# Graph network of four layers on one core: sort without messages and histogram, first and third layer with x stationary

## The chip, the cores and the metric

The kernel runs on one core of one Trainium2 chip. The metric is the device time of one execution in microseconds. TensorE (PE; PEld is its weight load), VectorE (DVE), ScalarE (ACT), GpSimd (POOL) and the DMA queue of SyncE (SP) work side by side and meet at semaphores.

## The reference

Four message-passing layers over 6250 nodes of 128 features and 200,000 edges. Each layer's result is added to x and layer-normalised.

```python
# layer 0: relation embedding, mean over incoming edges
msg = (x[src] + rel_emb[type64]) @ W_msg.T + b_msg
agg = segment_sum(msg, dst) / maximum(segment_sum(1, dst), 1)
x = layernorm(x + x @ W_self.T + b_self + agg)
# layer 1: four-head attention, sums over edges with row = src, col = dst
val_exp = exp(val - mx[src]) * edge_weight
agg = segment_sum(val_exp * h_neigh[dst], src) / segment_sum(val_exp, src)
x = layernorm(x + (norm(h_self) + norm(agg)) / 2)
# layer 2: two edge types, each with its own weights
msg = where(type2 == 0, x[src] @ W_data.T + b_data, x[src] @ W_control.T + b_control)
x = layernorm(x + relu(segment_sum(msg, dst) + x @ W_self.T + b_self))
# layer 3: symmetric normalisation with self loops
x = layernorm(x + segment_sum(norm * (x @ W.T + b)[dst], src))
```

## The kernel before, in words

Nodes lie in 49 tiles (NT) of 128. A sort routes the edge records into chunks of 128, one for each pair (source tile, destination tile), 49 x 49, and one spare chunk for each source tile (NX = 50 columns in a row of `recs`). No layer gathers: from the 128 records of a chunk, DVE compares place numbers with an iota and gets one-hot matrices, PE multiplies two of them into a 128x128 count table of the pair, ACT copies the table out of PSUM, and PE multiplies table and node features into the sums. A layer has seven batches of seven tiles (G7, NB); after each batch its `node` steps (dense products, norms) are dealt out over the next batch's loop, the last batch's stand behind the loop.

- Sort (block ahead of `aggregate_shared`, L234 to L723): 226 units of up to 32 chunk columns, 49 of the first level and 177 behind. In a unit DVE makes one-hots `O` (L582), `M` (L688), `rank` (L592), values `VO` (L701) and the permutation `PM` (L87); PE counts (L463, L466) and routes (L482); ACT copies (`R` L367, `place` L376, `recs`). Beside it run: the out-degree histogram (`sources`, `sides`: ten columns in each of the first 157 units), and from unit 77 on `linear`, which turns x into messages x @ W_msg.T + b_msg, split into three bf16 parts in `X`.
- Relation, layer 0 (`aggregate_own`, k = 1): for each of 50 destination steps 8 loops over 6 or 7 source tiles; per chunk a table matmul (L1765), a 64-column relation matmul (L1862) and a 384-column matmul with the table stationary and X moving (L1865). The tables go to HBM over a ring of 4.
- Weighted, layer 1 (k = 2): 49 rows x 8 loops; per chunk three table matmuls (L1761) and a float32 sum of 132 columns in two passes (L1867). The spare chunk has a table of its own: 50 tables in a row.
- Typed, layer 2 (k = 3): tables of all edges come back from HBM, ACT turns them into fp32r (L1711); per chunk one new table (L1765), one 258-column and one 256-column fp32r matmul, both with the table stationary (L1867, L1882). The last batch's steps, the splits of the new x into `Xr`, and `split_last_states` stand behind the loop.
- Plain, layer 3 (`aggregate_plain_turned`): here x is stationary and seven tables of one source tile stream, 448 columns at a time (L2123).

Of the kernel before, what the change touches and what calls it, by code (L numbers as in the profile page):

```python
# [22 lines left out]

# [13 lines left out]
def gnn_four_layers_kernel(nc, t, out):  # L37
# [13 lines left out]

# [10 lines left out]
    QUARTERS = RING = 4  # L62
    LONGEST = max(NT * (r + 1) // QUARTERS - NT * r // QUARTERS for r in range(QUARTERS))
    tab_d = nc.dram_tensor("tables", (NX * QUARTERS, P, LONGEST * P), BF16, kind="Internal").ap()

    with ExitStack() as ctx:
# [47 lines left out]
        relx = sb("relx", [P, 3, P], BF16)  # L114
        relw = sb("relw", [REL, P + 1], F32)
# [3 lines left out]
        ROW = 2 * P + 2  # L119
# [7 lines left out]
        spare = early[:, 2 * RC:]  # L127
# [7 lines left out]
        with ExitStack() as c1:  # L135
            raw = recs[:, :, :].bitcast(I32).rearrange("p c w -> p (c w)")
            psrc, pdst, esrc, edst = [raw[:, j * COLS:(j + 1) * COLS] for j in range(4)]
            turn_at = recs[:, :, :].rearrange("p c w -> p (c w)")[:, RC * 4 - COLS:RC * 4]
            ts_p = recs_h.rearrange("p c h -> p (c h)")[:, RC * 8 - 4 * COLS:RC * 8 - 2 * COLS].rearrange("p (c b) -> p c b", b=2)
# [21 lines left out]
            side = sb("side", [P, 2, 16, P + 2], BF16, c1)  # L161
            ts_hot = sb("ts_hot", [P, 2, 16, NTE], BF16, c1)
            dego = sb("dego", [NT, P], F32, c1)
            degx = sb("degx", [NT, P + 1], F32, c1)
            degs = sb("degs", [P, NT], F32, c1)
            valid = sb("valid", [P, 2], F32, c1)
            total_of = sb("total_of", [P, 1], F32, c1)
            junk = side[:, :, :, :].rearrange("p h n w -> p (h n w)")
            WT = sb("WT0", [P, 2, P], F32, c1)
            wnat = sb("wnat0", [P, 3, P], F32, c1)  # L170
            relT = sb("relT0", [P, REL], F32, c1)
            bias = sb("bias0", [P, 2, P], F32, c1)
            rel_r = sb("rel_r0", [REL, P], F32, c1)
            xT = sb("xT0", [P, P], F32, c1)
            msg = sb("msg0", [P, P], F32, c1)
# [3 lines left out]
            pL = ps("pL", [P, 3, P], c1)  # L179
# [4 lines left out]
                     "s_outhot", "s_side", "s_dego", "s_outadd", "s_deg", "s_tp0", "s_xt0", "s_y0", "s_lin0", "s_link0", "s_wt0", "s_valid", "s_total", "s_kind")  # L184
            (loads, pads, consts, tri_made, prep, fields, blanks, weighed, s_pad, s_load, s_xin, s_stored, turned, wt_made,
             s_dup, s_hot, s_cnt, s_look, s_mul, s_rank, s_more, s_pair, s_val, s_perm, s_out, s_ev,
             s_outhot, s_side, s_dego, s_outadd, s_deg, s_tp, s_xt, s_y, s_lin, s_link, s_wt, s_valid, s_total, s_kind) = [sem(n, c1) for n in names]
# [25 lines left out]
            SIDES = 10  # L213
            COUNTED = -(-COLS // SIDES)
            pieces_of = {n: (n * SIDES, min(SIDES, COLS - n * SIDES)) for n in range(COUNTED)}
            done_with = {u.d: n + 1 for n, u in enumerate(units) if u.level == 3}
            assert COUNTED < done_with[7] and 8 * TOP * NX * 8 <= RC * 8 - 4 * COLS
            LIN, LIN_AT = 7, A_N + 28
            assert LIN_AT + 3 * NT + 1 <= UN
            PREP, FIELDS, WEIGHED = 15, 9, 4  # L220
            PADDED = 96

            def slot_of(n):
# [1957 lines left out]
```

## Time and profile before

| | us |
|---|---|
| median of 3 runs | 4517.38 (4517.27 to 4522.35) |
| the profiled execution | 4517.95 |
| its span | 4516.2 |
| PE / PEld busy | 3879.5 (86%) / 3400.8 (75%) |
| DVE busy | 3899.9 (86%) |
| ACT busy | 2636.9 (58%) |
| POOL busy | 234.8 (5%) |

Busy time of an engine is the union of its instructions; neighbours on DVE and ACT overlap by about 0.08 us in the records, and matmuls overlap much more, since their ends are modelled. So PE is read by the distance from start to start. Shares over the whole span mix five stages with different limits; the rows below give them stage by stage.

### The profile page before, as it was taken

What the parts mean: (1) busy time and instruction counts of PE and PEld (TensorE: products, weight loads), DVE (VectorE), ACT (ScalarE), POOL (GpSimd) and SP (SyncE); (2) the same over time, 40 slices, a digit from 0 to 9 for tenths busy, and PEclk for the clock granted to TensorE, in tenths of its full rate; (3) what the DMA queues carried; (4) which work ended last, traced back from release to release, by engine and by line L of the source; (5) the groups of instructions that cost most, each with busy time, mean ns of one, the idle gap of its engine ahead of it and who ended that gap; (6) DMA issues with size and microseconds to landing.
All of it is one profiled execution on the core that took longest, in us unless ns stands there. A gap on an engine that the chain in (4) does not pass through costs nothing. (4 is left out here: it accounts for less than half of the span.)

```text
span 4516.2 us, 106596 instructions
## 1 busy us (share of the span) xinstructions
PE 3879.5 (86%) x43111; PEld 3400.8 (75%) x43112; DVE 3899.9 (86%) x6758; ACT 2636.9 (58%) x5471; POOL 234.8 (5%) x165
## 2 busy tenths in 40 slices
PE   3667777766679999995999999997999999969998
PEld 3556666555557666665999999997999999957776
DVE  8999999999988889986999999997666666669888
ACT  6878777843335555542333333333888888856776
POOL 1000001010100000000101011111000000000000
PEclk9989889989789999997999999998999999979999
DMA  3000000000013222220000000001333333300000
GB/s 106 1 1 2 1 2 2 2 2 1 2 51 122 112 109 114 108 108 2 2 2 2 2 2 2 2 2 34 106 98 97 98 97 97 97 5 5 10 9 9
DMA packets 92948, 183.53 MB, mean 41 GB/s; under 512 B 10329, under 2 KB 63781, under 8 KB 92322
## 3 DMA queue, kind: packets, MB, share of 16 engines
q1 hardware_dynamic: 91970, 174.17, 12.0%
q8 instruction: 351, 5.75, 0.5%
q10 hardware_dynamic: 480, 2.40, 0.2%
q14 instruction: 147, 1.20, 0.1%
HBM read 88.63 MB, written 87.90 MB: 39 GB/s over the span
## 5 line engine op out<-in xcount | busy, mean ns | idle before, releaser
L1720 ACT ACTIVATE gC<-qC 128x768 fp32r<-128x768 f32 (+3 forms) x792 | 653.4, 825 | 659.0 <-PE qC L1761 640.4
L87 DVE TENSOR_TENSOR g<-iota_own,recs 128x768 bf16<-128x768 bf16 (+1 forms) x1200 | 636.5, 560 | 177.2 <-PE qC L1765 171.1
L482 PE MATMUL pV<-VO,PM 128*128 128x98 bf16 (+4 forms) x6524 | 386.0, 225 | 326.8 <-issue 322.1
L1867 PE MATMUL qO<-A,gC 128*128 128x132 f32 x4900 | 637.0, 280 | 0.0
L482 PEld LDWEIGHTS pV<-VO,PM 128*128 128x128 bf16 x6524 | 356.4, 108 | 349.9 <-issue 348.9
L1867 PEld LDWEIGHTS qO<-A,gC 128*128 128x128 f32 x4900 | 581.3, 190 | 0.0
L1865 PE MATMUL qO<-terms,ring 128*128 128x384 bf16 x2450 | 523.7, 327 | 0.0
L1718 ACT ACTIVATE ring<-qC 128x768 bf16<-128x768 f32 (+1 forms) x400 | 328.8, 822 | 286.7 <-PE qC L1765 286.6
L87 DVE TENSOR_TENSOR PM<-iota_b,place 128x3584 bf16<-128x3584 bf16 (+1 forms) x226 | 469.8, 2079 | 14.7 <-ACT place L376 14.5
L414 ACT ACTIVATE side<-iota_b,recs 128x129 bf16<-128x129 bf16 x1568 | 475.6, 397 | 0.7 <-PE pD L492 0.7
L1862 PE MATMUL qO<-terms 128*128 128x64 bf16 x2450 | 470.2, 193 | 0.0
L87 DVE TENSOR_TENSOR places_hot<-iota_own,recs 128x896 bf16<-128x896 bf16 x700 | 403.1, 620 | 54.4 <-PE tC L2111 21.7
L2093 ACT ACTIVATE tables_r<-tC 128x896 fp32r<-128x896 f32 x350 | 320.7, 918 | 146.3 <-PE tC L2111 145.6
L1882 PE MATMUL qA<-Xr,kept_r 128*128 128x256 f32 x2450 | 386.8, 294 | 2.9 <-ACT kept_r L1711 2.9
L1711 ACT ACTIVATE kept_r<-sl_f 128x768 fp32r<-128x768 bf16 (+1 forms) x400 | 343.3, 858 | 77.2 <-PE qO L1867 63.2
L2123 PE MATMUL tO<-tables_r,Xr 128*128 128x448 f32 x1400 | 372.6, 388 | 9.0 <-ACT tables_r L2093 4.7
L1248 DVE TENSOR_TENSOR g<-sl_f 128x2304 bf16<-128x2304 bf16 (+1 forms) x262 | 369.9, 1412 | 0.2 <-PE qC L1761 0.2
L701 DVE TENSOR_TENSOR VO<-O,V 128x2744 bf16<-128x2744 bf16 (+3 forms) x226 | 362.5, 1604 | 3.6
L1867 PE MATMUL qO<-Xr,gC 128*128 128x258 f32 x2450 | 364.3, 285 | 1.1 <-ACT gC L1720 1.1
L1761 PE MATMUL qC<-g,sl_f 128*128 128x128 bf16 x4914 | 319.4, 220 | 47.9 <-DVE g L1248 46.9
L1865 PEld LDWEIGHTS qO<-terms,ring 128*128 128x128 bf16 x2450 | 239.2, 98 | 134.8 <-issue 0.7
L1761 PEld LDWEIGHTS qC<-g,sl_f 128*128 128x128 bf16 x4914 | 294.3, 98 | 59.4 <-DVE g L1248 54.6
(268 smaller groups left out, 6740.5 us busy)
## 6 DMA issues: line engine op xcount, KB each, us to landing
sl_f<-tables SPq DMA_DIRECT2D x350, 192.0 KB, 2.3
tables<-ring SPq DMA_DIRECT2D x150, 384.0 KB, 2.3
tables<-ring SPq DMA_DIRECT2D x50, 416.0 KB, 2.4
sl_f<-tables SPq DMA_DIRECT2D x50, 224.0 KB, 2.5
edges<-terms SPq DMA_DIRECT2D x1, 4312.0 KB, 13.5
B<-in_x SPq DMA_DIRECT2D x1, 2744.0 KB
out<-B SPq DMA_DIRECT2D x7, 392.0 KB
terms<-in_edge_type ACTq DMA_DIRECT2D x2, 686.0 KB
```

Source lines behind the costliest of these rows:

```text
L87: return v.tensor_tensor(o.rearrange("p n (a b) -> p n a b", b=2), (iota_own if own else iota_b)[:, at:at + w].rearrange("p (a b) -> p a b ...
L414: ins = act.activation(side[:, n % 2, j, 0:P + 1], iota_b[:, 0:P + 1], ACT.Sign, bias=turn_at[:, at + j:at + j + 1])
L482: mm = pe.matmul(pV[n % 2][:, g * row:(g + 1) * row].rearrange("p (f b) -> p f b", f=u.nf), PM[:, n % 2, col, :], values[:, :, col, :], st ...
L701: v.tensor_tensor(VO[:, n % 2, 0:cols * u.nf * u.w].rearrange("p (f n a b) -> p f n a b", b=2, a=u.w // 2, f=u.nf), where.unsqueeze(1).bro ...
L1248: ins = v.tensor_tensor(h1[:, par, 0:n, :, :].rearrange("p n s (a b) -> p n s a b", b=2), bare[Q % 3][:, 0:n, 1, :].rearrange("p n (a b) - ...
L1720: act.activation(Cs[:, u % 2, 0:n, :], pC[u % 2][:, 0:n, :], ACT.Copy).then_inc(s_cs, 1)
L1761: mm = pe.matmul(pC[u % 2][:, j, :], bare[G % 3][:, j, 0, :], h1[:, q % NHB, j, s, :], start=s == 0, stop=s == 2)
L1862: pe.matmul(pO[i % SUMS][:, parts * P:parts * P + P // 2], h2[:, q % NHB, j, :], h3[:, q % NHB, j, :], start=first, stop=last, skip_group_ ...
L1865: mm = pe.matmul(pO[i % SUMS][:, 0:width], table_j, x, start=False, stop=last, skip_group_check=True)
L1867: mm = pe.matmul(pO[i % SUMS][:, 0:width], table_j, x, start=first, stop=last)
L1882: mm = pe.matmul(pA[:, :], kept_r[:, q % 2, a - cut[q], :], Xr[:, a, 0:2 * P], start=a == 0, stop=a == NT - 1)
L2123: mm = pe.matmul(pO[:, h, 0:HW], Xr[:, b % NT, s * P:(s + 1) * P], table_h[:, h, :], start=b == 0 and s == 0, stop=b == NX - 1 and s == 1, ...
```

## The change

- Sort: `linear`, `relations`, `sources`, `sides` and `degrees` go. `X` holds x itself in three bf16 parts, made seven tiles at a time by ACT (`high_part`, `mid_part`) and POOL (`low_parts`). x @ W_self.T + b_self + x comes wholly from PE, and ACT copies it to `B`. The spare chunk of a row moves to its first column.
- Relation: new function with 343 units (7 batches x 49 source tiles). In a unit PE makes the tables of 7 destination tiles, the spare chunk adding into the first one's, streams them past `X` (three parts, stationary), and counts relations and types with 65-column matmuls. W_msg is applied to the sums in `node`, the relation counts times `relw` too. The out-degrees are summed by the ACTIVATE that copies the tables (`accum_out`).
- Weighted: 7 loops of 7 tiles in a row in place of 8; the spare chunk shares a table, so there are 49 sums in place of 50.
- Typed: like plain, with x (two fp32r parts) stationary; tables of all edges and of type 1 stream, 512 and 384 columns. The copies to fp32r are shared by DVE and ACT. The sums are already turned and go into the dense products as they are. The splits of batches 0 to 5 move into the loop of the last batch.
- Plain keeps its loop but for the column order. The table ring is 5 pieces of 224 KB. The SBUF reserve for dynamic DMA is 2048 bytes.

```diff
-                    def linear(n, step):
...
-                            v.tensor_tensor(msg[:, :], pL[:, 1, :], bias[:, 0, :], ALU.add).then_inc(s_lin, 1)
-                            v.tensor_tensor(own_x, own_x, pL[:, 2, :], ALU.add).then_inc(s_lin, 1)
...
-                        equal(v, ts_hot[:, n % 2, 0:cols, :], ts_p[:, at:at + cols, :], cols, NTE).then_inc(s_outhot, 1)
+                        gp.tensor_tensor(xrest[:, :, :], B[:, T, :], X[:, T, 0, :], ALU.subtract).then_inc(s_rest, 1)
+                        gp.wait_ge(s_mid, m + 1)
+                        gp.tensor_tensor(X[:, T, 2, :], xrest[:, :, :], X[:, T, 1, :], ALU.subtract).then_inc(s_low, 1)
...
+        def aggregate_relation_turned():
...
+                            equal_both_own(v, both_hot[:, U % 3, 0:n, :, :], places_of(chunk, n), n, P).then_inc(s_hot, 1)
...
+                            equal(v, rel_hot[:, K % 2, 0:n, 0:REL], rel_p[:, rel_at(m, a):rel_at(m, a) + n, :], n, REL, own=True).then_inc(s_rel, 1)
...
+                            act.activation(kept[U % RING].rearrange("p (n d) -> p n d", d=P), pC[U % 2][:, 0:G7, :], ACT.Copy, accum_out=sent[:, m, a:a + 1]).then_inc(s_cs, 1)
...
+                                for s in range(3):
+                                    mm = pe.matmul(pO[:, h, 0:(hi - lo) * P], X[:, a, s, :], of_half(kept[U % RING], h),
+                                                   start=a == 0 and s == 0, stop=a == NT - 1 and s == 2, skip_group_check=True)
...
+                                mm = pe.matmul(pR[:, to:to + DW], both_hot[:, U % 3, j, 0, :], rel_hot[:, K % 2, a % FOUR * n + j, 0:DW],
...
+                                        pe.matmul(pN[:, j - lo, :], A[:, m * G7 + j, 0:P], WTm[:, :], start=True, stop=False, skip_group_check=True)
+                                        mm = pe.matmul(pN[:, j - lo, :], RT[0:REL, j - lo, :], relw[:, :], start=False, stop=True, skip_group_check=True)
...
+        def aggregate_typed_turned():
...
+                            pe.wait_ge(s_kept[U % 2], U // 2 + 1) if whole else pe.wait_ge(s_cs, 2 * U + 2)
...
+                                for s in range(2):
+                                    mm = pe.matmul((pA if whole else pK)[:, h, 0:(hi - lo) * P], Xr[:, a, s * P:(s + 1) * P], of_half((all_r if whole else some_r)[:, U % 2, :], h),
...
+                        convert(0)
+                        for U in range(AHEAD):
+                            make(U)
...
+    nc = _bacc.Bacc("TRN2", target_bir_lowering=False, num_devices=1, dynamic_dma_scratch_size=2048)
```

DVE in the first level of the sort, one unit and the start of the next, before and then of the change:

```order
L701 TENSOR_TENSOR VO<-O,V 128x3584
L87 TENSOR_TENSOR PM<-iota_b,place 128x4096
L87 TENSOR_TENSOR ts_hot<-iota_b,recs 128x500
L688 TENSOR_TENSOR M<-O,R 128x448
L582 TENSOR_TENSOR O<-iota,V 128x448
L592 TENSOR_REDUCE rank<-M 128x32
```

```order
L656 TENSOR_TENSOR VO<-O,V 128x3584
L88 TENSOR_TENSOR PM<-iota_b,place 128x4096
L646 TENSOR_TENSOR M<-O,R 128x448
L606 TENSOR_TENSOR O<-iota,V 128x448
L616 TENSOR_REDUCE rank<-M 128x32
```

One row of six is gone. PE in the relation loop, before (the pair L1862 and L1865 stands once for each of 6 or 7 chunks) and then of the change, a whole unit and the start of a `node` step (rC and rO are the tables' and the sums' PSUM, rR the counts', sl_f the ring of tables, terms holds X):

```order
L1765 MATMUL qC<-terms,g 128x128 x6
L1862 MATMUL qO<-terms 128x64
L1865 MATMUL qO<-terms,ring 128x384
L1862 MATMUL qO<-terms 128x64
L1865 MATMUL qO<-terms,ring 128x384
```

```order
L1316 MATMUL rC<-both_hot 128x128 x7
L1328 MATMUL rO<-sl_f,terms 128x512 x3
L1328 MATMUL rO<-sl_f,terms 128x384 x3
L1343 MATMUL rR<-rel_hot,both_hot 128x65 x7
L1372 MATMUL rN<-ident_f,terms 64x128 x3
```

The narrow matmuls, which stood between wide ones, now stand seven in a row behind six wide ones.

## Rows read from the trace of the kernel before

**Rows 1.** Windows by stage: length, busy time and instructions of each engine, PE clock, DMA.
```profile
44.00:1301.00 1257.00, 873.00 (x11217) 734.06 (x11217) 1197.87 (x1797) 828.28 (x3020) 87.90 (x39) 0.89 0.03 8
...
1309.00:2026.00 717.00, 691.12 (x7733) 499.17 (x7733) 645.87 (x1655) 374.89 (x546) 0.00 (x0) 1.00 0.29 114
2026.00:2090.00 64.00, 12.44 (x45) 8.33 (x43) 30.94 (x48) 9.75 (x20) 9.32 (x6) 0.53 0.02 5
2090.00:3106.00 1016.00, 995.95 (x12250) 979.13 (x12250) 978.28 (x1014) 363.85 (x465) 106.01 (x96) 1.00 0.01 2
...
3134.00:3963.00 829.00, 823.11 (x7882) 797.20 (x7882) 533.15 (x1279) 673.73 (x951) 0.00 (x0) 1.00 0.36 99
3963.00:4017.00 54.00, 20.16 (x88) 14.29 (x88) 25.91 (x56) 16.66 (x32) 0.00 (x0) 0.61 0.00 1
```
**Rows 2.** Groups of DVE by line in 44 to 1301: busy, mean ns, idle before.
```profile
L688 DVE TENSOR_TENSOR M<-O,R 128x448 bf16<-128x448 bf16 (+2 forms) x226 | 83.9, 371 | 23.9 <-ACT R L367 23.7
...
L87 DVE TENSOR_TENSOR ts_hot<-iota_b,recs 128x500 bf16<-128x500 bf16 (+1 forms) x157 | 65.7, 419 | 0.0
L624 DVE TENSOR_TENSOR msg<-pL,bias 128x128 f32<-128x128 f32 x49 | 13.8, 283 | 3.7 <-PE pL L520 3.6
```
**Rows 3.** Timeline of DVE, a unit of the sort: start, length, instruction.
```profile
253.07 0.41 DVE L87 TENSOR_TENSOR ts_hot<-iota_b,recs 128x500 bf16<-128x500 bf16 x1
253.40 0.38 DVE L688 TENSOR_TENSOR M<-O,R 128x448 bf16<-128x448 bf16 x1
```
**Rows 4.** Timeline of PE in the sort, at full and at half clock.
```profile
1102.56 1.43 PE L482 MATMUL pV<-VO,PM 128*128 128x98 bf16 x28 [2.81 <-issue]
...
1285.28 2.12 PE L482 MATMUL pV<-VO,PM 128*128 128x84 bf16 x28 [2.56 <-issue]
...
1287.52 1.82 PE L466 MATMUL pR<-O,ones_b 128*128 128x364 bf16 x13
```
**Rows 5.** Timeline of GpSimd and VectorE where both work in the sort.
```profile
844.27 4.37 POOL L308 TENSOR_SCALAR beyond<-recs 128x200 bf16<-128x200 bf16 x1 [73.84 <-ACT recs L405]
...
1290.94 1.07 DVE L688 TENSOR_TENSOR M<-O,R 128x392 bf16<-128x392 bf16 x1
```
**Rows 6.** Timeline of PE in the relation loop, of PEld in the sort.
```profile
1708.27 0.19 PE L1862 MATMUL qO<-terms 128*128 128x64 bf16 x1
...
1708.46 0.52 PE L1765 MATMUL qC<-terms,g 128*128 128x128 bf16 x6
1708.81 0.19 PE L1862 MATMUL qO<-terms 128*128 128x64 bf16 x1
...
605.09 1.15 PEld L482 LDWEIGHTS pV<-VO,PM 128*128 128x128 bf16 x28 [0.91 <-issue]
```
**Rows 7.** Groups of DVE in the weighted stage, both one-hots of 6 and 7 chunks.
```profile
L93 DVE TENSOR_TENSOR sl_f<-iota_own,recs 128x1536 bf16<-128x1536 bf16 x194 | 185.9, 958 | 16.7 <-PE qC L1761 15.2
...
L93 DVE TENSOR_TENSOR sl_f<-iota_own,recs 128x1792 bf16<-128x1792 bf16 x66 | 71.7, 1087 | 7.3 <-PE qC L1761 6.5
```
**Rows 8.** Timeline of PE: dense product; typed loop, table to table; plain loop.
```profile
3972.00 1.16 PE L1792 MATMUL qN<-nWT,nxT 128*128 128x128 f32 x8
...
3403.44 0.50 PE L1765 MATMUL qC<-g 128*128 128x128 bf16 x6
...
3405.26 0.51 PE L1765 MATMUL qC<-g 128*128 128x128 bf16 x6
...
4290.13 0.56 PE L2111 MATMUL tC<-places_hot 128*128 128x128 bf16 x7
4290.51 1.06 PE L2123 MATMUL tO<-tables_r,Xr 128*128 128x448 f32 x4
4291.41 0.56 PE L2111 MATMUL tC<-places_hot 128*128 128x128 bf16 x7
```
**Rows 9.** Timeline behind the typed loop: VectorE adds the last dense product.
```profile
3985.11 0.54 DVE L1524 TENSOR_TENSOR A<-A,qN 128x384 f32<-128x384 f32 x1
```
**Rows 10.** DMA issues of the page: KB each, us from issue to landing.
```profile
sl_f<-tables SPq DMA_DIRECT2D x350, 192.0 KB, 2.3
```

More of the change, by code:

```diff
@@ L315, in _ @@
+                    gp.wait_ge(s_kind, n_kind)
                 @block.scalar
@@ L1045, in aggregate_own @@
-                if mode == "typed":
-                    kept = [sl_f[:, b * most * P // 2:(b + 1) * most * P // 2].bitcast(BF16).rearrange("p (n d) -> p n d", d=P) for b in range(RING)]
-                    kept_r = sb("kept_r", [P, 2, most, P], F32R, c)
-                if mode != "relation":
-                    Cs = sb(f"gC{name}", [P, 2, most, P], F32R if mode in ("plain", "typed") else cdt, c)
-                total = sb(f"total{name}", [P, 1, P], F32, c) if mode in ("relation", "plain") else None
@@ new lines, in node @@
+                            if slot == 43:
+                                after()
+                                step(v.tensor_tensor(Bt, Hn[:, :, :], W1[:, :, :], ALU.add))
+                        make_relations(0)
+                        for U in range(AHEAD):
+                            make(U)
+                        for U in range(UNITS):
+                            m, a = unit(U)
+                            if a == 0 and m > 0:
+                                close(m - 1)
+                            if U + AHEAD < UNITS:
+                                make(U + AHEAD)
+                                m2, a2 = unit(U + AHEAD)
+                                if a2 % FOUR == 0:
+                                    make_relations(pack_of(m2, a2))
+                            if m > 0:
+                                node(m - 1, a)
+                            elif a == 6:
+                                rows()
@@ L1891, in relations @@
-                        def relations(i):
-                            pe.wait_ge(s_reln, i + 1)
-                            if i >= 1:
-                                pe.wait_ge(s_total, 2 * i)
-                            pe.matmul(pE[:, 0:P + 1], rel_n[:, :], relw[:, :], start=True, stop=True).then_inc(s_relm, 1)
-                        table(0, 0)
-                        batch(0, None)
-                        for o in range(1, NB):
-                            batch(o, o - 1)
-                        if mode == "relation":
-                            turn_relations(TN - 1)
-                            relations(TN - 1)
@@ new lines, in node @@
+                                if slot == when + 4:
+                                    project(use + 2, hf, 1)
+                        table(0)
+                        for U in range(UNITS):
+                            m, a = unit(U)
+                            if U + 1 < UNITS:
+                                table(U + 1)
+                            sums(U)
+                            relations(U)
+                            if m > 0:
+                                node(m - 1, a)
+                            elif a == 7:
+                                weights()
@@ L1909, in softmax_weights @@
+                        for slot in range(44):
+                            node(NB - 1, slot)
         def softmax_weights():
@@ new lines, in _ @@
+                        for U in range(2):
+                            make(U)
+                        for U in range(UN):
+                            i, q = unit(U)
+                            m, slot = i // G7, U % (G7 * NQ)
+                            if U + 2 < UN:
+                                make(U + 2)
+                            if U + 2 == UN:
+                                recode()
+                            if q == 0 and i > 0:
+                                take(i - 1)
+                            if m > 0:
+                                node(m - 1, slot)
+                            else:
+                                degrees(slot)
```

1861 lines of the change are left out of this document (962 added, 899 removed).

## The prediction

> **What bounds the kernel now.** I read the windows by stage first, since the five stages have different limits, then the groups and waits of the sort, then PE's timeline in each loop. The windows [rows 1] say: in the sort (44 to 1301 us) DVE is busy 1198 of 1257 us, PE 873, ACT 828: DVE sets the pace, and 59 us of it is waiting, the largest part for `R` from ACT, 24 us [rows 2], that is for the chain PE route, PE count, ACT copy. In the relation loop (717 us) PE shows 691 us and DVE 646; in the weighted loop (1016 us) PE 996 and DVE 978; in the typed loop (829 us) PE 823 and DVE only 533. Behind the relation and the typed loop stand 64 and 54 us in which no engine is half busy: the last batch's steps, one after the other. The reader is to see that every stage has one engine to save on: DVE in the sort, PE in the typed loop, both at once in the other two.
>
> **The sort.** The histogram's one-hot is made in 157 units at 419 ns [rows 2]; neighbours overlap, and from its start to the next instruction's it is 0.33 us [rows 3], so 157 x 0.33 = 52 us. `linear` takes seven instructions of DVE for each of 49 tiles; the first is 283 ns [rows 2], with an overlap of 0.08 (0.41 - 0.33, [rows 3]) 0.20 net, and the short ones among them less, so 343 x 0.19 = 65 us. The few steps on relations and degrees give 3 us. Together 120 us of the engine that bounds. PE loses 1568 small matmuls and ACT as many `side` copies, neither of which is the bound, so that is worth nothing by itself. What is late next is the chain through PE. At full clock it routes 28 columns in 1.43 us, at half clock in 2.12, and counts in 1.82 there [rows 4]. At half clock 2.12 + 1.82 + the first count 0.5 + ACT's copy 0.5 + some 0.1 us for each of four hand-overs makes 5.3; a DVE unit of the later levels shrinks to about 4.5. So each unit at half clock now costs up to 0.8 us of new waiting. PE's clock is 0.89 in this window [rows 1], which is the half level 22% of the time: 226 x 0.22 x 0.8 = 40 us at most beside what is waited already, 0 at least; I take 15, since the units with waiting today already hold part of it. The seven 896-element copies twice on ACT (0.9 us each) stand in its slack, and PE's one matmul more per tile too. Sort: -120 + 15 = -105.
>
> GpSimd gets 14 subtractions of 896 floats beside DVE. Where both worked, one `M` took 1.07 us in place of 0.38 [rows 5, 3], while GpSimd's own instruction stretched to 4.37 us: it is mostly GpSimd that gives way. 14 x 0.7 = 10 us at most; I take 2, in the 15 above. The Trainium skill (SBUF — State Buffer, Who interferes with whom) states that a VectorE instruction with two inputs in SBUF and a GpSimd instruction that reads SBUF exclude each other for a whole instruction. If GpSimd always came first that would be a rival, below.
>
> **The relation loop.** Now 343 units of 7 tiles. Tables: six take from 1708.46 to 1708.81 [rows 6], 0.058 each, so 0.41 us. X stationary: 3 x (512 + 384) = 2688 columns; today 448 columns with two weight loads take 0.19 us (1708.27 to 1708.46), 0.424 ns a column, so 1.14 us. Seven 65-column matmuls: no trace of such a row of them. Bounds are the column rate, 0.027 each, and the table's 0.058; the nearest is the sort's weight loads, 28 in 1.15 us [rows 6], (1.15 - 0.10) / 27 = 0.039, which I take: 0.27 us. Unit 1.82 us (1.74 to 1.96), x 343 = 624 us, and 5 for the spare columns. `node` on PE: a dense product of float32 is (1.16 - 0.28) / 7 = 0.126 per pass, two passes [rows 8], 0.25 us; a batch has 14 of them today, and 14 more with `WTm` and `relw`, 7 transposes more, bias rows: 9.5 us, x 6 = 57. Sum 686 us. Today the same count gives 400 x 1.52 + 31 + 18 for the 50 relation products = 657, against 717 measured: 60 us lost to DVE's bursts. DVE drops: per unit one one-hot of 1792 (1.087 us [rows 7], net 1.0) and a quarter of another, 1.25 us, with node some 550 us of 700; but its node slots of 2.3 us against PE's 1.82 still come four at a time. I take 25 us lost (5 to 60). ACT's copy of 0.92 us and reading the accumulator, which no row shows, have 0.9 us of slack. Loop 686 + 25 = 711: -6 (-50 to +40).
>
> Behind the loop stand `keep`, the added transposes and products before the first norm: about 13 us in place of 7, and GpSimd clears one more array before: +7.
>
> **The weighted loop.** 343 pairs of DVE instructions replace 392. By rows [rows 7] 256 elements more cost 0.129 us, so what an instruction costs beside its elements is net 1.087 - 1792 x 0.000504 - 0.08, about 0.10 us; 98 fewer are 10 us, and PE's 49 sums fewer 49 x 0.23 = 11 us. Both engines that bound shrink by the same: -10 (-15 to -2).
>
> **The typed loop.** Today six tables and twelve sums of 256 to 258 columns go from 3403.44 to 3405.26 [rows 8]: 1.82 us. After: four sums of 512 and four of 384 for seven tiles. In the plain loop four sums of 448 take 0.90 us (4290.51 to 4291.41), 0.226 each with the change from bf16 to fp32r in it. Both rows fit a cost of 0.055 for that change, once for a unit, and 0.211 for 448 columns, 0.12 for 257: 0.48 ns a column, so 0.242 and 0.180. Four pairs 1.69, the change 0.055, seven tables 0.39: 2.10 us after rounding down, since the trace of the plain loop has single steps of 0.205. Bounds: the bf16 rate 0.424 gives 1.91, 0.226/448 gives 2.20. x 343 = 720, spare columns 3, `node` on PE 9 us a batch, 54, waits of the short buffers 8: 785. So -44 (-105 to +5). DVE has 1.0 for one-hots, half a convert and node, about 1.7 us of 2.1; ACT two halves and half a convert, 1.5: both hidden.
>
> Behind it: today the chains of turn and product last until 3985.11 [rows 9], 22 us, with six splits queued into the 10 us behind. After, two chains of transpose and three products, about 10 us, and no splits but one: 54 - 19 = 35 us, -19 (-10 to -26). Its start waits for the first table, since `convert(0)` stands ahead of `make`: the DMA's 2.3 us [rows 10] and the copy, +3.
>
> **Sum.** -105 - 6 + 7 - 10 - 44 - 19 + 3 = -174. The plain stage and the softmax between are not changed. The profiled execution took 4517.95, 0.6 above the median of the runs, which is nothing here; 4518 - 174 = 4344. I say 4342.
>
> **Rivals.**
> - The TensorE clock stays low in the sort. With less work PE idles more, and at half clock the chain of 5.3 us becomes the unit in most units: 226 x about 0.5 more = 110 us, and the sort gains about 10. 4440. For it: the clock already falls with some 30% idle. Against: at half clock PE is busy nearly throughout, and the half level lasts 3 or 4 us at a time today, in which DVE keeps on. 6%.
> - The relation loop gets worse: narrow matmuls at 0.058, DVE's bursts at today's 60 us: 343 x 0.13 + 35 = +80. 4422. For: seven narrow ones in a row have never been seen here. 8%.
> - GpSimd first: all 14 subtractions hold DVE for their length. By DVE's kind of float32 work on 896 elements at 1.1 us and GpSimd two to four times slower, 14 x 3 = 42 us more: 4384. This is what the page's rule on the shared port would do at its worst. 5%.
> - Slower than before: the tables' DMAs go one by one. Both turned loops need one piece of 224 KB for each unit, in 1.82 and 2.10 us, while landing takes 2.3 us for 192 KB [rows 10]. If the smaller reserve let only one be in flight, with issue 0.3 and landing 2.4 a unit would take 2.7 us and more; it decides from 1.82 on, costs 2 x 343 x 0.75 = 510 us, less the slack, and gives 4850. For it: the diff lowers that reserve. Against: the queue is of the hardware kind and was at 114 GB/s with 0.29 of the engines [rows 1]; the new rate is 120. 3%.
> - It doesn't do what it says: the typed loop stays bound by something else at 829. 4386. 4%, as DVE and ACT would both have to be 20% above my count.
>
> **Chances.** Forecast 4342, 74%; the rivals 6, 8, 5, 3 and 4%. Adding the parts' better and worse ends independently gives about -55 and +60 around the forecast; the worse cases of the rivals reach to 4440. Range 4285 to 4405, which leaves out about 2 in 10. A difference under 0.2% (9 us) is no change that the runs can tell. Faster by more: 95%; within it: 1%; slower: 4%, the DMA case and what I haven't thought of.
>
> **What would show it.** In the profile after: the sort ends near 1195 us; a DVE unit of its first level takes 5.27 us in place of 5.60 (start of `M` to start of `M`); the relation loop's unit is near 1.85 us between `node` steps and its 65-column matmuls start 0.04 us apart; the typed unit is 2.1 us, its 512-column sums start 0.24 apart; typed to plain 35 us; the weighted loop about 1006. I am wrong if DVE's wait for `R` grows past 60 us, if ACT in the relation loop waits for `tables`, or if the one-hots come late to the tables.

## The result and the profile after

The changed kernel takes 4362.97 us in the median of four runs (4352.71 to 4366.67), the kernel before 4517.59. The ratio on record is 0.9652, 95% interval 0.9634 to 0.967; the two medians divided give 0.9658. The forecast was 4342 with a range of 4285 to 4405. The profiled execution is the shortest of the four, 4352.71 with a span of 4351.0, so what it lost against before in span is 165.2 us, ten more than the medians say.

First the windows by stage of the changed kernel, with the columns of [rows 1] (start and end, length, busy time and instructions of PE, PEld, DVE, ACT, POOL, clock, DMA share, GB/s):

```profile
44.00:1185.70 1141.70, 757.41 (x9742) 640.47 (x9742) 1099.54 (x1280) 418.87 (x1510) 144.03 (x98) 0.90 0.03 8
...
1200.30:1930.90 730.60, 697.91 (x7404) 479.95 (x7404) 557.57 (x678) 395.07 (x802) 105.93 (x89) 1.00 0.29 110
...
2002.70:3003.00 1000.30, 980.38 (x12152) 966.94 (x12152) 969.88 (x917) 350.60 (x417) 81.39 (x96) 1.00 0.01 2
...
3035.20:3820.40 785.20, 783.19 (x5643) 652.97 (x5644) 543.95 (x765) 524.11 (x978) 0.00 (x0) 1.00 0.34 101
```

For before I cut the sort at the start of its last routing matmul and the loops at their first and last matmul in the same way:

```profile
44.00:1297.80 1253.80, 871.74 (x11213) 733.08 (x11213) 1196.63 (x1791) 827.78 (x3016) 86.20 (x36) 0.89 0.03 8
1309.10:2026.10 717.00, 691.22 (x7733) 499.19 (x7733) 645.84 (x1655) 374.89 (x546) 0.00 (x0) 1.00 0.29 114
...
3134.10:3962.60 828.50, 823.03 (x7882) 797.20 (x7882) 532.77 (x1276) 673.73 (x951) 0.00 (x0) 1.00 0.36 99
```

Stage by stage, in us of the two profiled executions, beside what was forecast:

| from ... to | before | after | difference | forecast |
|---|---|---|---|---|
| start to the first table of the relation loop | 1309.1 | 1200.3 | -108.8 | -105 |
| relation loop | 717.0 | 730.6 | +13.6 | -6 |
| behind it | 64.0 | 71.8 | +7.8 | +7 |
| weighted loop | 1015.9 | 1000.3 | -15.6 | -10 |
| weighted to typed | 28.1 | 32.2 | +4.1 | +3 |
| typed loop | 828.5 | 785.2 | -43.3 | -44 |
| behind it | 54.7 | 32.8 | -21.9 | -19 |
| plain stage | 498.9 | 497.8 | -1.1 | 0 |
| sum | | | -165.2 | -174 |

Seven of the eight rows are within 6 us, and the typed loop is right to one. The relation loop alone is on the wrong side, by 20 us: it got longer. And the first row is right as a sum and wrong inside, as the experiments below show.

Now the groups of DVE in the sort of the changed kernel (busy, mean ns, idle before and its releaser), the answer to [rows 2]:

```profile
L88 DVE TENSOR_TENSOR PM<-iota_b,place 128x3584 bf16<-128x3584 bf16 (+1 forms) x226 | 472.0, 2088 | 0.0
L656 DVE TENSOR_TENSOR VO<-O,V 128x2744 bf16<-128x2744 bf16 (+3 forms) x226 | 371.9, 1645 | 5.1
...
L646 DVE TENSOR_TENSOR M<-O,R 128x448 bf16<-128x448 bf16 (+2 forms) x226 | 90.4, 400 | 21.9 <-ACT R L396 21.7
```

And the same engine before, two groups that [rows 2] does not hold:

```profile
L87 DVE TENSOR_TENSOR PM<-iota_b,place 128x3584 bf16<-128x3584 bf16 (+1 forms) x226 | 469.8, 2079 | 14.7 <-ACT place L376 14.5
L701 DVE TENSOR_TENSOR VO<-O,V 128x2744 bf16<-128x2744 bf16 (+3 forms) x226 | 362.5, 1604 | 3.6
```

Two things are to be seen. The same instructions have become longer: M 90.4 us in place of 83.9, VO 371.9 in place of 362.5. And a wait is gone: PM waited 14.5 us for ACT's `place`, now nothing. The wait of M for `R`, on which I had put the loss, is 21.7 us in place of 23.7.

PE in the relation loop, timeline (start, length, instruction), a unit and one `node` step:

```profile
1317.04 1.30 PE L1328 MATMUL rO<-sl_f,terms 128*128 128x512 bf16 x6
1318.17 0.39 PE L1343 MATMUL rR<-rel_hot,both_hot 128*128 128x65 bf16 x7
1318.40 0.46 PE L1378 MATMUL rN<-WTm,A 128*128 128x128 f32 x2
1318.79 0.48 PE L1379 MATMUL rN<-relw,terms 64*128 64x128 f32 x2
1319.21 0.49 PE L1378 MATMUL rN<-WTm,A 128*128 128x128 f32 x2
...
1320.88 0.56 PE L1316 MATMUL rC<-both_hot 128*128 128x128 bf16 x7
1321.28 1.30 PE L1328 MATMUL rO<-sl_f,terms 128*128 128x512 bf16 x6
1322.41 0.38 PE L1343 MATMUL rR<-rel_hot,both_hot 128*128 128x65 bf16 x7
1322.63 0.55 PE L1316 MATMUL rC<-both_hot 128*128 128x128 bf16 x7
```

A unit without `node` takes 1.75 us (1320.88 to 1322.63): 0.40 for tables, 1.13 for the six wide sums, 0.22 for the seven narrow ones, all inside the bounds of the forecast. Between `node` products it is different: each group of two passes starts 0.41 to 0.42 us behind the one before, so one pass costs 0.207 us on average, where the forecast had 0.126. PE in the typed loop, timeline:

```profile
3301.24 0.56 PE L2064 MATMUL rC<-both_hot 128*128 128x128 bf16 x7
3301.62 1.06 PE L2076 MATMUL rK<-some_r,Xr 128*128 128x512 f32 x4
3302.51 0.98 PE L2076 MATMUL rA<-all_r,Xr 128*128 128x512 f32 x4
3303.34 0.56 PE L2064 MATMUL rC<-both_hot 128*128 128x128 bf16 x7
```

A unit is 2.10 us, as forecast. Last, GpSimd and VectorE where one of GpSimd's new subtractions runs, timeline of the changed kernel:

```profile
365.96 1.95 POOL L314 TENSOR_TENSOR xrest<-B,terms 128x896 f32<-128x896 f32 x1 [327.54 <-ACT terms L450]
366.09 0.55 DVE L616 TENSOR_REDUCE rank<-M 128x28 f32<-128x392 bf16 x1
366.56 2.80 DVE L656 TENSOR_TENSOR VO<-O,V 128x2744 bf16<-128x2744 bf16 x1
```

VO takes 1.57 us where GpSimd is still. It began at 366.56, GpSimd's instruction ended at 367.91, and 2.80 is longer by 1.23: VectorE stood until about then. The reduction before it, which reads one tensor, kept its 0.55. Over the 14 subtractions the instruction with two inputs beside each is 1.04 to 1.69 us longer, 18.9 us in all.

### The profile page after: what moved, and what is told of

Same layout as the page of the kernel before. It is cut to its first block and busy times, and to the rows that moved or that the text cites. A ratio compares the mean times of both kernels' runs of the same rounds, so it can differ in the third digit from the quotient of the medians.

```text
span 4351.0 us, 94545 instructions
## 1 busy us (share of the span) xinstructions
PE 3717.3 (85%) x38991; PEld 3134.1 (72%) x38992; DVE 3708.3 (85%) x4644; ACT 2074.6 (48%) x4187; POOL 381.5 (9%) x320
## 5 line engine op out<-in xcount | busy, mean ns | idle before, releaser
L94 DVE TENSOR_TENSOR both_hot<-iota_own,recs 128x1792 bf16<-128x1792 bf16 (+1 forms) x686 | 756.8, 1106 | 252.2 <-PE rR L1343 142.5
L1690 ACT ACTIVATE gC<-qC 128x896 f32<-128x896 f32 x343 | 314.8, 918 | 647.9 <-PE qC L1710 647.9
L2034 ACT ACTIVATE some_r<-rC 128x512 fp32r<-128x512 f32 (+1 forms) x686 | 336.4, 543 | 253.1 <-PE rC L2064 252.6
L1328 PE MATMUL rO<-sl_f,terms 128*128 128x512 bf16 (+1 forms) x2058 | 446.6, 353 | 4.0 <-ACT sl_f L1294 2.4
L1294 ACT ACTIVATE sl_f<-rC 128x896 bf16<-128x896 f32 x343 | 314.1, 916 | 279.6 <-PE rC L1316 279.4
L656 DVE TENSOR_TENSOR VO<-O,V 128x2744 bf16<-128x2744 bf16 (+3 forms) x226 | 371.9, 1645 | 5.1
L1528 DVE TENSOR_TENSOR g<-sl_f 128x2688 bf16<-128x2688 bf16 (+1 forms) x229 | 363.6, 1588 | 0.2 <-PE qC L1710 0.2
L2076 PE MATMUL rK<-some_r,Xr 128*128 128x512 f32 (+1 forms) x1372 | 363.2, 386 | 0.0
L2076 PE MATMUL rA<-all_r,Xr 128*128 128x512 f32 (+1 forms) x1372 | 342.0, 371 | 1.9 <-DVE all_r L1835 1.9
L507 PE MATMUL pR<-O,ones_b 128*128 128x392 bf16 (+16 forms) x2644 | 301.3, 267 | 0.0
L507 PEld LDWEIGHTS pR<-O,ones_b 128*128 128x128 bf16 x2644 | 242.7, 105 | 79.8 <-issue 20.1
```

The lines of the kernel that those rows point to most:

```text
L94: return v.tensor_tensor(o.rearrange("p n k (a b) -> p (n k) a b", b=2), iota_own[:, 0:w].rearrange("p (a b) -> p a b", b=2).unsqueeze(1). ...
L507: mm = pe.matmul(pR[n % 2][:, (j + 1) * row:k].rearrange("p (m r) -> p m r", r=row), ones_b[:, :], O[:, n % 2, j * row:(j + 1) * row].unsq ...
L656: v.tensor_tensor(VO[:, n % 2, 0:cols * u.nf * u.w].rearrange("p (f n a b) -> p f n a b", b=2, a=u.w // 2, f=u.nf), where.unsqueeze(1).bro ...
L1328: mm = pe.matmul(pO[:, h, 0:(hi - lo) * P], X[:, a, s, :], of_half(kept[U % RING], h), start=a == 0 and s == 0, stop=a == NT - 1 and s == ...
L1528: v.tensor_tensor(h1[:, U % 2, 0:n, :, :].rearrange("p n s (a b) -> p n s a b", b=2), bare[U % 3][:, 0:n, 1, :].rearrange("p n (a b) -> p ...
L2034: act.activation(of_half(some_r[:, U % 2, :], h).rearrange("p (n d) -> p n d", d=P), pC[Q % 3][:, 0:hi - lo, :], ACT.Copy).then_inc(s_cs, 1)
```

## Experiments

Differences are of medians. Runs of the changed kernel are read against its own repeat, runs of the kernel before against the kernel before beside them. The runs stood on three chips, and the kernel before took 4517.67 us beside after_again and the three n_ runs, 4518.34 beside s_low, s_kind, b_noside and b_nohot, and 4519.54 beside the rest. So a difference to the repeat on another chip holds to some 2 us at best.

**after_again: the changed kernel once more.**

> The changed kernel once more, so that the three next to it are read against it on the same chip: 4353 to 4367 us as in its first four runs. Relation loop 730 us, from the first table's matmul to the last narrow one.

Measured 4362.63 us (4359.66 to 4366.91); ratio 0.9659 (0.9646 to 0.9672). The relation loop took 730.5 us, all later stages agree to 1 us but for the step from typed to plain (34.6 in place of 32.8), and the sort was 6.2 us longer than in the first profile. So of the 7 us between these two profiles 6 are variation in the sort.

**n_padded and n_grouped: why a `node` product costs 0.41 us.** The first lets the products with relw run over 128 rows, in the old order (the add that fills relw keeps to its first 64 rows, which isn't shown):

```diff
-        relw = sb("relw", [REL, P], F32)
+        relw = sb("relw", [P, P], F32)
...
+                        v.memset(relw[REL:P, :], 0.0)
+                        v.memset(RT[REL:P, :, :], 0.0)
...
-mm = pe.matmul(pN[:, j - lo, :], RT[0:REL, j - lo, :], relw[:, :], start=False, stop=True, ...)
+mm = pe.matmul(pN[:, j - lo, :], RT[:, j - lo, :], relw[:, :], start=False, stop=True, ...)
```

> The products with relw run over all 128 rows (64 of them zero on both sides), in the old order, alternating with WTm. Theory S (rows change): passes fall from 0.207 to 0.126 us, 28 products by 0.16 us by 7 batches = -31 us at most where PE is what bounds, -20 to -30. Theory A (accumulation into the same region) and theory P (fixed price): 0.

The second changes only the order, in each half of a batch. It changes the sums that are formed in that bank too; only its time is used.

```diff
                                     for j in range(lo, hi):
                                         pe.matmul(pN[:, j - lo, :], A[:, m * G7 + j, 0:P], WTm[:, :], start=True, stop=False, ...)
+                                    for j in range(lo, hi):
                                         mm = pe.matmul(pN[:, j - lo, :], RT[0:REL, j - lo, :], relw[:, :], start=False, stop=True, ...)
```

> The 14 pairs of products of node in the relation loop (A by WTm with 128 rows, RT by relw with 64 rows) stand in pairs and take 0.413 us each in the trace, 0.207 for each of the two passes, while the dense products that follow each other take 0.126 for a pass. Here all products with WTm of a half come first, then all with relw. Theory S (the change between 128 and 64 rows costs, since the next weights can't load beside the running product): a batch has 28 products of which 24 no longer follow a change, each 0.16 us cheaper, 3.9 less four starts left, about -2 to -2.5 us a batch, -13 to -17 us in all. Theory A (accumulating behind a write to the same PSUM region costs): the same here. Theory P (such a product simply costs 0.41, whatever stands before it): 0.

n_padded: 4344.77 us (4340.72 to 4348.98), -17.9; n_grouped: 4347.45 (4342.77 to 4349.19), -15.2; both 0.9621 (0.9608 to 0.9634). Theory S had said -20 to -30 for the first, which it misses, and -13 to -17 for the second. PE in n_padded, timeline:

```profile
1314.60 0.46 PE L1380 MATMUL rN<-WTm,A 128*128 128x128 f32 x2
1314.90 0.39 PE L1381 MATMUL rN<-relw,terms 128*128 128x128 f32 x2
1315.13 0.39 PE L1380 MATMUL rN<-WTm,A 128*128 128x128 f32 x2
1315.35 0.39 PE L1381 MATMUL rN<-relw,terms 128*128 128x128 f32 x2
```

Each group of two passes starts 0.22 to 0.23 us behind the one before, 0.112 for a pass, in the same order and with twice the rows. That puts theory A (a price of adding to the same region) out, and also a fixed price for a product that adds. It leaves a rival: a pass over 64 rows might be dear in itself, and n_padded has none. PE in n_grouped settles that, timeline:

```profile
1325.31 0.91 PE L1378 MATMUL rN<-WTm,A 128*128 128x128 f32 x6
1326.15 0.93 PE L1380 MATMUL rN<-relw,terms 64*128 64x128 f32 x6
1327.01 0.56 PE L1316 MATMUL rC<-both_hot 128*128 128x128 bf16 x7
```

Six passes over 64 rows in a row take 0.86 us, hardly more than six over 128 (0.84): within the row they too start 0.112 us apart. So it is the change that costs, and once for each change: two passes behind a change take 0.41 us in place of 0.22, which is 0.19 us, or 0.09 on average for a pass. The weight loads show where it goes, PEld in the changed kernel and then in n_padded:

```profile
1318.79 0.29 PEld L1379 LDWEIGHTS rN<-relw,terms 64*128 64x128 f32 x2
```

```profile
1314.79 0.30 PEld L1381 LDWEIGHTS rN<-relw,terms 128*128 128x128 f32 x2
```

Behind a change of rows the load starts together with its matmul (1318.79, as in the rows above); without one it starts 0.11 us ahead of it (1314.79 against 1314.90), beside the matmul that still runs.

Counted so, a batch has 14 changes, none in n_padded and 4 in n_grouped: 98 by 0.19 are 18.6 us and 70 by 0.19 are 13.3. From the first table of the relation loop to the start of the weighted loop n_padded is 16.3 us shorter than the repeat and n_grouped 13.4. Both expectations had counted a batch's 28 passes as 28 products, so that n_grouped came out within its range by luck. The loop itself shrank from 730.5 to 716.6 us in n_padded, and what stands behind it from 72.1 to 69.6. In n_grouped a pass costs 0.14 on average.

**n_deep: the idle time of PE in the relation loop.**

```diff
-                both_hot = sb("both_hot0", [P, 3, G7 + 1, 2, P], BF16, c)
+                both_hot = sb("both_hot0", [P, 4, G7 + 1, 2, P], BF16, c)
...
-            AHEAD, FOUR = 2, 4
+            AHEAD, FOUR = 3, 4
```

(and the buffer's index modulo 4, the wait for its release one unit later)

> Four buffers of both_hot in place of three in the relation loop, and VectorE one unit further ahead. PE idles 33 us in this loop, in a batch 0.7 us in slot 12, 1.3 in slot 36 and 1.1 in slot 44, where VectorE's steps of node are in a row. Theory B (bursts longer than the lead): the lead grows by a unit of 1.74 us, the three gaps close nearly, -6 x 2.8 = -17 us (-10 to -20). Rival (VectorE is late for lack of throughput over the stretch, or held by its own wait for PE's products): at most -4 us.

4338.47 us (4327.84 to 4341.41), -24.2; 0.9598 (0.9585 to 0.9611). What PE waited for in the relation loop, of the changed kernel and of n_deep (us, times, longest):

```profile
PE rC L1316 <- DVE both_hot L94: 38.7, 32, 12.1
PE rO L1328 <- ACT sl_f L1294: 2.4, 6, 0.4
```

```profile
PE rC L1316 <- DVE both_hot L94: 16.7, 13, 11.9
PE rO L1328 <- ACT sl_f L1294: 8.6, 12, 1.2
```

The first 12 us of each are the way into the loop. Without them the idle time falls from 29 to 13 us. The whole gain is past the -10 to -20 of theory B, which went by the idle time that the profile shows. The loop is 24.1 us shorter, more than the idle time that went: the rest stands in the row of narrow matmuls, which from start to next start take 92.3 us in the changed kernel and 84.6 here. A wait shorter than the modelled length of the last matmul (0.19 us) is not told as idle. The lead was too short for VectorE's steps of `node`; its throughput was not the limit (557 of 730 us busy).

**s_low, s_kind: which of GpSimd's new work holds VectorE.**

```diff
-                        gp.tensor_tensor(xrest[:, :, :], B[:, T, :], X[:, T, 0, :], ALU.subtract).then_inc(s_rest, 1)
+                        gp.memset(xrest[:, :, :], 0.0).then_inc(s_rest, 1)
...
-                        gp.tensor_tensor(X[:, T, 2, :], xrest[:, :, :], X[:, T, 1, :], ALU.subtract).then_inc(s_low, 1)
+                        gp.memset(X[:, T, 2, :], 0.0).then_inc(s_low, 1)
```

> The changed kernel, in which GpSimd's 14 subtractions of 896 floats (the middle and low parts of X) are writes of zeros, so the middle and low parts are left out. VectorE's five instructions of a sort unit are 22 us longer in sum after the change than before (M 90.4 against 83.9 us, VO 371.9 against 362.5, PM 2.2, the first step on over-full groups 3.3). Theory L (it is the subtractions that hold VectorE): the sum falls back by 15 to 20 us. Theory K (it is GpSimd's 48 small additions to the relation numbers): by at most 5 us. Total -15 or -5 us against 4363.

```diff
-                        for a in range(n):
-                            gp.tensor_tensor(later[:, :, lo + a, :, :], ... , ALU.add).then_inc(s_kind, 1)
+                        gp.memset(later[:, :, lo:hi, :, :].rearrange("p m a c b -> p m (a c b)"), 0.0).then_inc(s_kind, 1)
```

> The changed kernel, in which GpSimd's 49 small additions that lay out the relation numbers of batches 1 to 6 are seven writes of zeros, so these relation numbers are left out. Theory K: VectorE's sum in the sort falls by 10 to 20 us. Theory L: by at most 5.

s_low: 4343.50 us (4341.11 to 4345.68), -19.1; 0.9613 (0.9597 to 0.9629). s_kind: 4368.41 (4365.48 to 4372.42), +5.8; 0.9668 (0.9652 to 0.9684). VectorE in the sort of s_low:

```profile
L656 DVE TENSOR_TENSOR VO<-O,V 128x2744 bf16<-128x2744 bf16 (+3 forms) x226 | 362.8, 1605 | 5.1
...
L646 DVE TENSOR_TENSOR M<-O,R 128x448 bf16<-128x448 bf16 (+2 forms) x226 | 85.5, 378 | 27.1 <-ACT R L396 27.0
```

With GpSimd's subtractions gone, VO is back at its time of before. It is the 14 wide subtractions and not the 49 small additions. Theory L stands: beside GpSimd's writes of zeros no VectorE instruction of s_low is longer than elsewhere. That s_kind came out 6 us slower was expected by neither theory. The intervals of its ratio and of the repeat's overlap, so this may be noise; in its profile VectorE waits 35 us for `R` in place of 24, and PE is at half clock for 290 us of the sort in place of 253. Why that should be so stays open.

**s_dve, s_pieces: the same subtractions elsewhere.** s_dve gives the two lines, unchanged but for the engine, to VectorE behind `PM`, at units 2 and 7 of each eight.

```diff
+                            m, when = divmod(n - SPLIT_AT, 8)
+                            if 0 <= m < NB and when == 2:
...
+                                v.tensor_tensor(xrest[:, :, :], B[:, T, :], X[:, T, 0, :], ALU.subtract).then_inc(s_rest, 1)
```

> The changed kernel with the 14 subtractions of X's parts on VectorE (after PM of units 2 and 7 of each eight) in place of GpSimd. In the profile each of GpSimd's takes 1.9 us and the VectorE instruction beside it is 1.1 to 1.7 us longer, 19 us in sum. Theory L (GpSimd's instruction holds VectorE's two-input instruction nearly for its whole length): on VectorE itself they cost 14 x 1.0 = 14 us, so 5 us less than now in the sort, 4350 to 4362. If GpSimd's had cost nothing, as my prediction had it: 14 us more, 4377.

s_pieces leaves them with GpSimd in seven pieces each:

```diff
+                        for i in range(G7):
+                            ins = gp.tensor_tensor(xrest[:, i:i + 1, :], B[:, m * G7 + i:m * G7 + i + 1, :], X[:, m * G7 + i:m * G7 + i + 1, 0, :], ALU.subtract)
+                        ins.then_inc(s_rest, 1)
```

> The changed kernel with each of GpSimd's 14 subtractions in seven of 128 floats. Theory L1 (the port passes at the end of each instruction of either engine, so a short one holds VectorE shortly, and VectorE's next goes on): VectorE's longest delay falls from 1.7 to about 0.3 us, but up to seven of them follow each other, sum 7 to 19 us in place of 19, total -5 (-12 to 0). Theory L2 (the two simply share reads by halves): no change in VectorE's sum.

s_dve: 4356.60 us (4351.97 to 4357.93), -6.0; 0.964 (0.9627 to 0.9653). s_pieces: 4352.09 (4349.96 to 4353.93), -10.5; 0.963 (0.9617 to 0.9643). On VectorE, the busiest engine of the stage, the subtractions seem to cost less than on the idle GpSimd: a subtraction takes 1.08 us there, and VectorE is busy for 1096 us of the sort in place of 1102 in the repeat. But the intervals of s_dve and the repeat overlap, and so do those of s_dve and s_pieces. s_pieces alone is clear of the repeat. The timeline of s_pieces has two kinds of stretch, first this one:

```profile
365.80 15.11 POOL L315 TENSOR_TENSOR xrest<-B,terms 128x128 f32<-128x128 f32 x7 [327.02 <-ACT terms L454]
366.40 1.56 DVE L660 TENSOR_TENSOR VO<-O,V 128x2744 bf16<-128x2744 bf16 x1
...
367.89 2.01 DVE L88 TENSOR_TENSOR PM<-iota_b,place 128x3584 bf16<-128x3584 bf16 x1
```

Here it is GpSimd that waits: seven pieces take 15.11 us, and VO and PM keep their 1.56 and 2.01. It is the only group of seven like this. The other 13 take 6.0 to 9.2 us, and VectorE is held in each:

```profile
388.85 6.63 POOL L319 TENSOR_TENSOR terms<-xrest,terms 128x128 bf16<-128x128 f32 x7 [7.94 <-ACT terms L460]
389.47 0.58 DVE L650 TENSOR_TENSOR M<-O,R 128x392 bf16<-128x392 bf16 x1
...
392.42 2.24 DVE L88 TENSOR_TENSOR PM<-iota_b,place 128x3584 bf16<-128x3584 bf16 x1
```

M takes 0.34 elsewhere and PM 2.01, so each is 0.23 or 0.24 longer. Over all 14 groups up to six instructions in a group are longer, none by more than 0.24 us, and the sum is 13.1 us in place of 18.9. That is theory L1 with its numbers (up to seven short delays of some 0.3, 7 to 19 us in sum); L2 (no change in VectorE's sum) is out. The 5.8 us saved on VectorE are about half of the 10.5 in the median; for the rest no run shows a cause. Nor does one show why the first group left VectorE alone.

**b_noside, b_nohot, b_both: the two halves of the histogram, in the kernel before.**

```diff
-                        for j in range(cols):
+                        for j in range(cols if n < 2 else 1):
                             ins = act.activation(side[:, n % 2, j, 0:P + 1], iota_b[:, 0:P + 1], ACT.Sign, bias=turn_at[:, at + j:at + j + 1])
```

> The kernel before, with one of ten side copies of ACT in each histogram unit after the second (about 1400 of 1568 left out, so the histogram is wrong), all VectorE and PE instructions as they are. My prediction counted ACT's part of the histogram at nothing: 4517. Rival theory: ACT's queue makes VectorE wait for place, 14.5 us before, which is gone after the change; then VectorE's wait before PM falls from 14.7 to under 3 us and the time to about 4505.

```diff
-                        equal(v, ts_hot[:, n % 2, 0:cols, :], ts_p[:, at:at + cols, :], cols, NTE).then_inc(s_outhot, 1)
+                        equal(v, ts_hot[:, n % 2, 0:(cols if n < 2 else 1), :], ts_p[:, at:at + (cols if n < 2 else 1), :], cols if n < 2 else 1, NTE).then_inc(s_outhot, 1)
```

> The kernel before, with VectorE's one-hot of the histogram cut to one column in each unit after the second (so the histogram is wrong). VectorE bounds the sort: 155 x (0.33 - about 0.10) = 36 us less, 4481. If the chain PE to ACT bounded instead: about 4510.

> The kernel before, with both cuts to the histogram: ACT's side copies (alone -18 us) and VectorE's one-hot (alone -13 us where VectorE had 30 us less to do), so the histogram is wrong. Theory C (the two engines are links of one cycle, VectorE's saving was eaten by waiting for ACT's place and R): together more than the sum, -40 to -50. Theory H (half clock: VectorE's saving is eaten by PE's chain at 1.2 GHz): the sum or less, -25 to -31.

The first expectation is met (4505 of the rival theory, not 4517). The second is not: 4481 was expected, and its other case, the chain PE to ACT with 4510, came nearer. b_noside: 4500.63 us (4495.45 to 4502.92), -17.7; 0.9958 (0.9941 to 0.9975). b_nohot: 4505.48 (4504.36 to 4507.9), -12.9; 0.997 (0.9958 to 0.9981). b_both: 4478.77 (4477.1 to 4483.82), -40.8; 0.991 (0.9897 to 0.9924). VectorE's `PM` in b_noside, the window of b_both's sort, and VectorE's waits in the sort of b_nohot and then of b_both (us, times, longest):

```profile
L87 DVE TENSOR_TENSOR PM<-iota_b,place 128x3584 bf16<-128x3584 bf16 (+1 forms) x226 | 470.3, 2081 | 0.2 <-ACT place L376 0.2
```

```profile
44.00:1257.70 1213.70, 859.50 (x11212) 721.67 (x11213) 1163.50 (x1788) 444.81 (x1623) 70.81 (x36) 0.90 0.03 8
```

```profile
DVE M L688 <- ACT R L367: 32.9, 44, 2.6
DVE PM L87 <- ACT place L376: 17.6, 38, 0.9
```

```profile
DVE M L688 <- ACT R L367: 26.9, 34, 2.6
DVE msg L624 <- PE pL L520: 6.0, 13, 1.2
```

Taking ACT's copies away gave 17.7 us, though ACT had been busy for only 828 of 1254: VectorE's wait for `place` is gone, and its idle time (length minus busy, sort) fell from 57 to 38 us. Taking 30 us of work from VectorE gave 12.9, since its idle time rose to 72 us. Both together gave 40.8, more than the 30.6 of the two apart, with the idle time at 50. The total is at the low edge of theory C and 10 us beyond theory H, but by the intervals of the three ratios the difference between 40.8 and 30.6 is itself uncertain by some 11 us; the sorts of the profiles, 40.1 us shorter against 19.7 and 14.6, put it at 6. And the larger part of what came back does not hang on ACT's copies: without them, from b_noside to b_both, VectorE lost 33 us of work and the sort only 20, with M's wait for `R` growing from 19 to 27 us. So the two halves of the histogram do act on each other, by a few us, and the largest part of the waiting that ate VectorE's saving is for `R`. What makes `R` late (PE's clock, PE's work or ACT's order) these runs don't separate.

**best: three edits at once.** relw and RT over 128 rows, four buffers, the subtractions on VectorE, each as above.

> Three edits to the changed kernel at once: relw and RT padded to 128 rows, four buffers of both_hot, the 14 subtractions on VectorE. The first two gave -18 and -24 us against 4362.6; they are in one loop, but one saves PE's work and the other PE's waiting, so they add: 4320; with the third 4315 (4305 to 4325). If VectorE becomes the bound of that loop once PE is faster, only -30: 4332.

4313.64 us (4309.33 to 4317.01); 0.9543 (0.953 to 0.9556), against 0.9659 (0.9646 to 0.9672) of the changed kernel beside the same kernel before. Its relation loop takes 690.8 us (1202.1 to 1892.9). The gains add, as 4315 had it, and this is the fastest of all kernels here. s_pieces in place of s_dve wasn't tried in this combination.

## Why the prediction was right, point by point

- **Typed loop, -44:** -43.3. The terms hold one by one. From start to next start the 2744 wide sums on record cost 0.218 us on average, eight of them 1.74 (forecast 1.69 and 0.055 for the change of type), seven tables 0.39 (0.39). PE is busy 783 of 785 us, ACT and DVE are both hidden with 524 and 544.
- **Behind the typed loop, -19, and the start, +3:** -21.9 and +4.1 between weighted and typed.
- **Weighted loop, -10:** -15.6, just past the -15 that I gave as its end. The pieces are PE's sums, 582.6 us before and 567.0 after from start to next start; the tables are 413 in both.
- **Relation loop, -6:** +13.6. The unit was right: 142 + 390 + 92 us in 343 units are 1.82. **One step that failed is "`node` on PE: 9.5 us" a batch.** It has 72.9 us in the loop in place of 57. The 168 passes with WTm and relw cost 34.8 us, 0.207 each, where I had 0.126 from dense products that follow each other [rows 8]. n_padded and n_grouped show that the difference is the change between 64 and 128 rows. **The other is "60 us lost to DVE's bursts".** It is what a count of today's loop had left over (657 of 717); PE is busy 691 of the 717 us [rows 1], so the records show only 26 idle, and no 35 us of waiting to lose. PE's idle time rose to 33 us in place of the 25 that I took, since VectorE's lead was short (n_deep). So PE's busy time and its idle time each grew by 7. My own sign of being wrong, one-hots that come late to the tables, is there: 27 us in 31 waits behind the way in. The trace of before had a row for the first step: the product of relw with 64 rows between others of 128, which I did not set against the new pairs:

```profile
2021.61 0.49 PE L1896 MATMUL qE<-relw,rel_n 64*128 64x129 f32 x2
2022.02 0.20 PE L1862 MATMUL qO<-terms 128*128 128x64 bf16 x1
```

  From 2021.61 to 2022.02 it is 0.41 us for two passes. The Trainium skill (TensorE: Matmul & The Clock Gate, LDWEIGHTS (loading the stationary operand)) says that the time of a weight load goes by its columns and not by its rows. The trace agrees for the load itself, 184 ns with 64 rows and 189 with 128; what the runs add is that a change of rows costs 0.19 us beside it.
- **The sort, -105:** -108.8 with the way into the relation loop, and -102.8 in the repeat. That the sum came so close is luck: two errors of some 19 us each stood against each other. VectorE's busy time fell by 97 us and not by 120: **"it is mostly GpSimd that gives way ... I take 2" failed**, it cost 19. The two rows that I read together [rows 5] are of different moments, and with what ran beside each the trace of before already showed both cases:

```profile
844.80 2.01 DVE L87 TENSOR_TENSOR PM<-iota_b,place 128x3584 bf16<-128x3584 bf16 x1
```

```profile
1289.76 2.03 POOL L310 TENSOR_TENSOR terms<-recs,beyond 128x400 bf16<-128x400 bf16 x1
```

  GpSimd's 4.37 us at 844.27 began while VectorE's VO ran, and VectorE lost nothing. The M of 1.07 us at 1290.94 stood beside this other instruction of GpSimd, which had begun first and wasn't stretched (2.03, its group has 2.24 on average); it ended at 1291.79 and M at 1292.01. The rival at 42 us was nearer; it had the mechanism and took each at 3 us in place of 1.4. Its "two to four times slower" no row shows; measured are 1.9 to 2.1 us on GpSimd against 1.08 on VectorE (s_dve). The Trainium skill (SBUF — State Buffer, Who interferes with whom) states that whoever issues first holds the shared ports for the whole instruction, that reductions are exempt and that instructions which only write do not lock. The runs agree in most: VO waits to the end of GpSimd's, the reduction beside it keeps 0.55, and s_low's writes of zeros delay nothing that shows (VO 362.8 as before). By that rule the forecast would have had the length of the 14 subtractions, 28 us at most. The first group of s_pieces doesn't follow from it: pieces that were issued before PM let it go ahead.
- **"PE loses 1568 small matmuls and ACT as many `side` copies, neither of which is the bound, so that is worth nothing" failed too:** b_noside is 17.7 us faster, by VectorE's wait for `place`, 14.5 us, which ended behind ACT's copies, and some 4 us of M's for `R`. What PE's 1568 matmuls were worth no run shows.
- **"+15 of new waiting" at half clock:** VectorE's idle time in the sort fell from 57 to 42 us. Of this 19 are what b_noside shows for ACT's copies, so some 4 us of new waiting are left for everything else. M's wait for `R` did not grow (21.7 after, 23.7 before). In b_nohot and b_both, where PE keeps its work, 15 us of a saving of 30 on VectorE (against before) and 12 of 33 (against b_noside) came back as waiting.
- **Rivals:** tables whose DMAs go one by one: of 224 KB a write lands in 1.9 us and a read in 2.5 (medians), the read in more than its unit (785 us for 343), so more than one was in flight, and no wait of PE inside the two turned loops is put down to a transfer. The clock stays as it was in the sort, 0.90 and 0.89.

## What to carry to other kernels

An engine with much idle time can still end a wait of the one that bounds: read who ended the waits of the bounding engine, and count what stands in that releaser's queue, before work there is called free. Work given to GpSimd beside a busy VectorE is not free where both read wide tensors: here 14 subtractions cost 19 us. Short pieces were cheaper, and so, within the noise, was VectorE itself. Two rows that are read as one event must be of the same moment. Before a duration of a matmul is carried over, look at what stands before it in the new order, its rows above all. What a count leaves over is not yet waiting: set it against the engine's idle time.

## What the hardware showed that was not expected

- A change between fp32 products over 128 and over 64 rows costs 0.19 us: alternating, a pass starts 0.207 us behind the one before; with the 64 padded with zeros to 128, 0.112 to 0.123; and 64-row passes in a row also 0.112. More rows of zeros were faster by 17.9 us in the whole kernel.
- One GpSimd subtraction of 896 floats took 1.9 to 3.2 us beside VectorE and held it for 1.0 to 1.7. Cut into seven of 128 floats, 13 groups of 14 took 6.0 to 9.2 us and held several VectorE instructions for at most 0.24 each; one group stretched to 15.11 us without delaying VectorE.
- 65-column bf16 matmuls, seven in a row with their weights, mostly start 0.029 to 0.036 us apart. ACT's accumulated copy shows as 0.92 us and a read of 0.19 behind it, together 1.1 us of a unit of 1.75.
